# First chunk pair of the first group as eight plain block products, with the sums of x and of the weights due later

## The reference

```python
def lora_add(base, inp, A, B):
    Ab = A[layer_idx][lora_indices]
    Bb = B[layer_idx][lora_indices]
    t = jnp.einsum('bri,bni->bnr', Ab, inp)
    return base + jnp.einsum('bor,bnr->bno', Bb, t) * SCALE
gate = lora_add(jnp.einsum('bnh,fh->bnf', x, W_gate), x, A_gate, B_gate)
up = lora_add(jnp.einsum('bnh,fh->bnf', x, W_up), x, A_up, B_up)
act = jax.nn.silu(gate) * up
down = lora_add(jnp.einsum('bnf,hf->bnh', act, W_down), act, A_down, B_down)
...
logits = x @ W_gate + b_gate
_, top_idx = jax.lax.top_k(logits, TOP_K)
y_all = jax.nn.relu(jnp.einsum('bsd,edh->bseh', x, W_e) + b_e)
y = jnp.take_along_axis(y_all, top_idx[..., None], axis=2)
return y.mean(axis=2)
```

## Time and profile before

| | |
|---|---|
| median of 3 runs | 1849.49 us (1849.46 to 1853.57) |
| the profiled execution, its own time | 1849.29 us |
| its span | 1847.4 us |
| PE busy | 1811.7 us, 98% of the span |
| DVE / ACT / POOL busy | 1252.5 / 751.6 / 1078.5 us |
| mean granted TensorE clock | 0.995 |
| DMA | 350.33 MB, 190 GB/s on average |

### The profile page before, as it was taken

How to read it: one execution, slowest core, us unless ns; L and a number is a source line. 1 busy time by engine, 2 the same in 40 slices (tenths; PEclk the granted TensorE clock), 3 DMA queues, 4 the chain that set the end, 5 groups by cost and what they waited for, 6 DMA issues and landing times.

```text
span 1847.4 us, 25090 instructions
## 1 busy us (share of the span) xinstructions
PE 1811.7 (98%) x8582; PEld 1507.1 (82%) x8582; DVE 1252.5 (68%) x1496; ACT 751.6 (41%) x1128; POOL 1078.5 (58%) x676
## 2 busy tenths in 40 slices
PE   7999999999999999999999999999999999999997
PEld 6788888888888888888888888888888888888886
DVE  8877788875567797888888886477788642234400
ACT  5544444444543335444444444443323333333332
POOL 2678888873434445545656553444433776676664
PEclk9999999999999999999999999999999999999999
DMA  5556665644667655565566665567635876577643
GB/s 211 173 200 225 223 205 202 234 171 147 208 230 249 223 181 184 174 195 179 179 201 210 191 207 189 191 232 243 219 117 180 244 192 145 141 193 186 157 103 47
DMA packets 128396, 350.33 MB, mean 190 GB/s; under 512 B 15232, under 2 KB 17152, under 8 KB 128000
## 3 DMA queue, kind: packets, MB, share of 16 engines
q1 hardware_dynamic: 110320, 286.94, 45.7%
q0 software_dynamic: 17952, 61.75, 14.3%
HBM read 267.49 MB, written 90.05 MB: 194 GB/s over the span
## 4 chain that ended last, share of the span: by engine, by line
PE 82%; POOL 8%; DMA 3%; DVE 3%; issue 2%; ACT 1%; SPq 0%; POOLq 0%; ACTq 0%; DVEq 0%
PE PS L1716 25%; PE PS L1717 25%; PE PS L1718 25%; PE PS L1831 2%; PE PS L2059 2%; PE PS L1758 2%; DMA FT<-in_wp 1%; POOL FT L719 1%; POOL ytp L715 1%; POOL FT L717 1%; POOL FT L693 1%; POOL brw L749 1%; POOL ytp L713 1%; POOL FT L688 1%; DMA X<-in_xp 1%
## 5 line engine op out<-in xcount | busy, mean ns | idle before, releaser
L1716 PE MATMUL PS<-R,ring 128*128 128x512 f32 (+1 forms) x1800 | 708.5, 394 | 18.7 <-DVE R L937 9.4
L1717 PE MATMUL PS<-R,ring 128*128 128x512 f32 (+1 forms) x1800 | 703.5, 391 | 0.0
L1718 PE MATMUL PS<-R,ring 128*128 128x512 f32 (+1 forms) x1800 | 702.6, 390 | 0.0
L1716 PEld LDWEIGHTS PS<-R,ring 128*128 128x128 f32 x1800 | 339.3, 189 | 88.6 <-issue 12.8
L1718 PEld LDWEIGHTS PS<-R,ring 128*128 128x128 f32 x1800 | 339.1, 188 | 72.0
L1717 PEld LDWEIGHTS PS<-R,ring 128*128 128x128 f32 x1800 | 339.7, 189 | 65.9
L770 POOL TENSOR_TENSOR ring<-raw,ring 128x1024 fp32r<-128x1024 f32 x78 | 192.7, 2471 | 267.7 <-ACT ring L893 267.6
L1716 PE MATMUL PS<-ring,R 128*128 128x512 f32 x592 | 231.7, 391 | 1.7 <-DVE FT L1234 1.7
L1717 PE MATMUL PS<-ring,R 128*128 128x512 f32 x592 | 230.8, 390 | 0.0
L1718 PE MATMUL PS<-ring,R 128*128 128x512 f32 x592 | 230.4, 389 | 0.0
L749 POOL DMA_INDIRECT brw<-in_bgu,idx_b x88 | 94.0, 1068 | 226.9 <-DVE R L1058 187.9
(11 more groups left out here) (189 smaller groups left out, 2365.8 us busy)
## 6 DMA issues: line engine op xcount, KB each, us to landing
raw<-in_wp SPq DMA_DIRECT2D x124, 512.0 KB
act_scratch<-FT SPq DMA_DIRECT2D x140, 256.0 KB, 5.0
FT<-act_scratch SPq DMA_DIRECT2D x70, 512.0 KB, 4.4
raw<-in_we SPq DMA_DIRECT2D x64, 512.0 KB
ytp<-in_wgb SPq DMA_DIRECT2D x96, 256.0 KB, 4.8
raw<-wt_scratch SPq DMA_DIRECT2D x40, 512.0 KB
out<-in_xn SPq DMA_DIRECT2D x17, 512.0 KB, 5.5
y_scratch<-FT SPq DMA_DIRECT2D x7, 1024.0 KB, 6.0
```

Source lines behind the costliest of these rows:

```text
L1716: e.matmul(out_, hi, whi, start=start, stop=False, skip_group_check=True)
L1717: e.matmul(out_, hi, wlo, start=False, stop=False, skip_group_check=True)
L1718: return e.matmul(out_, lo, whi, start=False, stop=stop, skip_group_check=True)
```

## The change

The first group's first chunk pair (q = 0) is made of eight plain block products, which need no sums at all, summed in PSUM: banks 0 and 1 take two products each with B11 and B21, banks 2 and 3 two each with B12 and B22. Gate results then lie complete in four banks; silu reads them there (`plain_silu`), and the four copies and four additions of this pair go. The other seven products of q = 1 follow after all eight. x is split in the order B11, B21, B12, B22, T1, T2, T3, T4; B12 lies in the place that T3 takes later, so the high part of T3 now waits until the plain products with B12 and `lora1_in(0, 1)` are through. `lora1_in(0, 1)` takes B12 and B22 (32 small matmuls) instead of T1, B11 and B22 (48). The third weight block is now issued after all of x. The due times of the first 14 slots are written in microseconds through `early`.

```diff
-X_FIRST = ["B11", "B21", "T1", "T2", "B22", "T3", "T4"]
+X_FIRST = ["B11", "B21", "B12", "B22", "T1", "T2", "T3", "T4"]
+PLAIN = [(0, "B11", 0), (1, "B21", 0), (2, "B11", 1), (3, "B21", 1), (0, "B12", 2), (1, "B22", 2), (2, "B12", 3), (3, "B22", 3)]
...
+def pos(g, q, j):
+
+    if g == 0:
+        return 7 * q + j if q >= 2 else 4 + j
...
+def early(us):
+
+    return (us - 9.4) / 3.57 - 1
...
-        sp.add(-23.5, load, 2)
+        sp.add(-20.5, load, 2)
...
             elif r == 5:
-                e.wait_ge(s_xl, 14)
+                e.wait_ge(s_xl, 16)
...
+            if g == 0 and o == "T3":
+                e.wait_ge(s_pe, 3)
+                e.wait_ge(s_t1, 2)
             if g == 0 and o == "T4":
                 e.wait_ge(s_xl, x_at(0, "T3", 1))
...
-        def mix_w0(e, q, part):
+        def mix_w0(e, part):
...
         def e_copy(e, g, q, k):
...
-            if q and k == 0:
+            if g == 0 and q == 1 and k < 2:
+                if k == 0:
+                    e.wait_ge(s_gl, 4)
+                    e.wait_ge(s_as, AS_FIRST)
+            elif q and k == 0:
                 e.wait_ge(s_c, c_of(g, q - 1, 2))
...
+        def plain_silu(e, k):
+
+            if k == 0:
+                e.wait_ge(s_p0, 1)
+                e.wait_ge(s_xp, 4)
+                e.wait_ge(s_xl, x_at(0, "T2", 1))
+            e.activation(tile(SG_T + k), PS[:, [0, 2, 1, 3][k], :], ACT.Silu).then_inc(s_c, 1)
...
+        W_HI = [5.4, 9.0, 12.3, 12.9, 21.8, 21.9, 26.6, 32.5, 36.0, 49.2, 49.3]
...
+        X_LO = {"B11": (7.5, 8.5), "B21": (10.5, 11.5), "B12": (14.0, 15.0), "B22": (16.5, 17.5),
+                "T1": (24.0, 24.1), "T2": (32.0, 32.1), "T3": (41.0, 41.1), "T4": (50.0, 50.1)}
...
-                src = ([("B11", 0), ("B21", 4)], [("T1", 0), ("B11", 0), ("B22", 4)])[w]
+                src = ([("B11", 0), ("B21", 4)], [("T1", 0), ("B11", 0), ("B22", 4)] if g else [("B12", 0), ("B22", 4)])[w]
...
+            def plain(i):
+
+                n, x, bank_ = PLAIN[i]
+                e.wait_ge(s_lo, lo_of(0, n))
+                m = main1(0, n, x, bank_, i % 2 == 0)
+                if i >= 4:
+                    m.then_inc(s_pe, 1)
...
             def first_pairs(g):
+                if g == 0:
+                    for i in range(4):
+                        plain(i)
+                    lora1_in(0, 0)
+                    for i in range(4, 8):
+                        plain(i)
+                    lora1_in(0, 1)
+                    lora1_out(0, 0, 0, 0, 0)
+                    lora1_out(0, 0, 1, 0, 1)
+                    product(0, 1, 0)
+                    product(0, 1, 1)
+                    lora1_out(0, 0, 0, 1, 2)
+                    lora1_out(0, 0, 1, 1, 3).then_inc(s_p0, 1)
+                    for j in range(2, 7):
+                        product(0, 1, j)
+                    return
```

More of the change, by code:

```diff
@@ L80, in pos, with when_at @@
     return 7 * q + j
-AT_POS = {pos(q, j): (q, j) for q in range(NP) for j in range(7)}
+def when_at(g, q, j):
+    return 7 + j if g == 0 and q == 1 else pos(g, q, j)
+def early(us):
+    return (us - 9.4) / 3.57 - 1
+AT_POS = [{pos(g, q, j): (q, j) for q in range(1 - g, NP) for j in range(7)} for g in range(2)]
 def op(g, n):
@@ L105, in piece_list @@
             n0 = op(g, 7 * q)
-            first, second = {0: (-6.0, -5.5), 1: (-12.7, -6.0)}.get(q, (-6.0, -5.5))
+            first, second = {0: (-6.0, -5.5), 1: (-12.7 if g else -12.3, -6.0)}.get(q, (-6.0, -5.5))
             out.append((n0 + first, ("w", g, 2 * q)))
@@ L261, in build @@
         s_v = sem("s_v")
+        s_p0 = sem("s_p0")
         s_m, s_oe = sem("s_m"), sem("s_oe")
@@ L592, in build @@
                     free = op(a, 148) - 4.7
+                elif a == 0 and q < 2:
+                    free = early([[11.5, 14.5], [36.5, 53.0]][q][c])
                 elif c:
-                    free = op(a, pos(q, 6)) - 4.7
+                    free = op(a, pos(a, q, 6)) - 4.7
                 else:
@@ L953, in x0_t3 @@
             e.wait_ge(s_xt, h + 1)
+            e.wait_ge(s_xl, x_at(0, "B12", h))
             e.wait_ge(s_q[6 + h], 16)
@@ L1343, in block0_lo @@
                             ALU.subtract).then_inc(s_tlo, 1)
+        W_HI = [5.4, 9.0, 12.3, 12.9, 21.8, 21.9, 26.6, 32.5, 36.0, 49.2, 49.3]
+        W_LO = [6.1, 10.0, 13.0, 13.1, 23.0, 23.1, 31.6, 39.5, 39.6, 48.5, 51.5]
+        X_HI = {"B11": (6.5, 7.5), "B21": (9.5, 11.0), "B12": (13.6, 14.6), "B22": (15.6, 16.6),
+                "T1": (22.0, 22.1), "T2": (30.5, 30.6), "T3": (40.0, 40.1), "T4": (47.0, 47.1)}
+        X_LO = {"B11": (7.5, 8.5), "B21": (10.5, 11.5), "B12": (14.0, 15.0), "B22": (16.5, 17.5),
+                "T1": (24.0, 24.1), "T2": (32.0, 32.1), "T3": (41.0, 41.1), "T4": (50.0, 50.1)}
         for g in range(NG):
             for n in range(LO1):
+                if g == 0 and n < 14:
+                    if n < 11:
+                        act.add(early(W_HI[n]), w_hi, 0, n)
+                        dve.add(early(W_LO[n]), w_lo, 0, n)
+                    continue
                 key = op(g, n) - (4.98 if g == 0 or n > 4 else 4.96 if n % 2 else 3.98)
+                if g == 0 and n < 20:
+                    key = n - 1.95 if n < 17 else 14.05 + 0.3 * (n - 17)
                 act.add(key, w_hi, g, n)
@@ L1396, in build @@
                 for k in range(4):
[L1397 to L1399 removed]
+                    if (g, q) == (0, 0):
+                        act.add(early(48.7 + 0.1 * k), plain_silu, k)
+                        continue
+                    key = 9.2 if g and q == 1 and k == 0 else when_at(g, q, [0, 2, 3, 5][k]) + 1.05
                     act.add(op(g, key), e_copy, g, q, k)
[L1401 removed]
+                    due = op(g, when_at(g, q, [4 if q < 2 else 1, 6, 6, 6][k]) + [1.1, 1.05, 1.1, 1.15][k])
                     dve.add(due, c_add, g, q, k)
@@ L1438, in build @@
         for h in range(2):
-            dve.add(-1.75 + 0.001 * h, x0_t1, h)
-            dve.add(-0.8 + 0.001 * h, x0_t2, h)
-            dve.add(1.2 + 0.001 * h, x0_t3, h)
-            dve.add(2.2 + 0.001 * h, x0_t4, h)
-        for q in range(2):
-            for part in range(3):
-                dve.add([[-1.5, 0.16, 1.16], [2.5, 2.51, 2.52]][q][part], mix_w0, q, part)
+            dve.add(early(20.5 + 0.1 * h), x0_t1, h)
+            dve.add(early(29.0 + 0.1 * h), x0_t2, h)
+            dve.add(early(37.0 + 0.1 * h), x0_t3, h)
+            dve.add(early(45.5 + 0.1 * h), x0_t4, h)
+        for part in range(3):
+            dve.add(early([26.5, 35.0, 35.1][part]), mix_w0, part)
         for k in range(8):
```

143 lines of the change are left out of this document (69 added, 74 removed).

## The result

The changed kernel took 1858.54 us (median of 6 runs, 1854.53 to 1860.3), the kernel before 1849.47 us beside it (6 runs, 1848.69 to 1853.57): ratio 1.0043, 95% interval 1.0029 to 1.0057. It is slower by about 9 us (by the interval, 5 to 11), 0.6 us over the forecast and inside the range. The profiled execution took 1860.3 us, its span is 1858.5 us. It is the slowest of the six, 1.8 us above their median, so what it shows late in the program need not be typical.

What follows compares the result with a forecast made beforehand. PE, busy 98%, bounds the kernel. The chain gave +8.4 us, PE's account (work +0.9, waits 16.0 against 7.6) +9.3; 8.6 was taken on 1849.29, forecasting 1857.9, with 1851.0 to 1862.0 for 8 in 10.

Steps and rivals of the forecast that it cites:

- PE's own work: Before q = 2: one more product, 2.75 us, and 16 fewer small adapter matmuls, minus 1.8; sum +0.9 us.
- First wait: Before the adapter's product: PE waits 1.8 us, until 23.9, for the adapter's low parts, now behind both halves of B22.
- Second and third: PE's waits before q = 2: 2.2 us for the B rows, until 50.4, and 1.0 us for product 4's copy, at 57.3.
- The chain: From the adapter product through T3, T4, ACT's silus to T4's low part at 61.9, then POOL's gather and last copy, 76.9.
- POOL's piece: From the start of q = 2's weight sums (63.4) to the gathered rows' high part (75.2): 11.8 us, unchanged.
- The clock: After PE's long wait before q = 2: 3.4 us at half rate, losing 1.7 us, the same price as before.
- Nothing later: Behind the long wait, later weight high parts and gathers are late by as much as PE and hold up nothing more.
- A: Faster: T4's low part by 50.9 us, last copy not late: 1845.0, or 1839.9 without the first three waits; chance 0.06.
- B: About the same: POOL's chain only half as late, T4 between 52 and 58: 1848 to 1855, typically 1852; chance 0.16.
- C: Slower still: gather for pairs 2 and 3 late, table switch with drain: +1 to +3, up to 1861.5; chance 0.10.
- D: Before q = 2: the third sum's copy isn't needed that early; rejected in the prediction, no size or chance given.

Runs made afterwards that it cites:

- the fastest version: Changed kernel with second row gather, silus, adapter's low parts and gathered rows moved, POOL's q = 2 weight sums held until T4: 1843.73 us, 0.9958 of kernel before.

## Why the prediction was right

**PE's own work, +0.9.** By PE's account the front grew by 6.6 us of waits and 0.8 us more lost to the clock, and 7.65 in all, so the rest is +0.3, 0.6 less than forecast. Some 0.45 of these are no work of the change: PE ended its first four products at 21.82 instead of 22.27, though they use the same blocks, because its first matmuls went over to the faster pace 0.9 us earlier in this execution (see the last section). So the term itself was about right.

**First wait.** Predicted 1.8 us and PE going on at 23.9; measured 2.01 and 23.83. The time at which PE goes on is the forecast that held; the length of the wait was 0.5 to 2.0 us in the seven profiles that share this stretch of the program, and PE went on at 23.8 to 23.9 in all of them.

**Second and third.** 2.2 at 50.4 and 1.0 at 57.3; measured 2.20 at 50.39 and 0.83 at 57.41.

**The chain.** First half of T3's high part at 45.9, measured 45.83; T4 written at 53.3, measured 53.33; ACT's split done at 54.4, measured 54.43; high part of the weight block 58.9, measured 58.8; T4's low part 61.9, measured 61.8. Every length was read off the same operation in the rows before, and the order from the due times. From the start of the table load to the start of the first silu it took 1.30 us, against 1.29 in the earlier trace rows. The Trainium skill ("ScalarE: Activation LUTs", What ACT_TABLE_LOAD costs) adds a drain of 1.38 us, which is in neither trace, though ACT had just ended a split (52.23 + 2.20 = 54.43) when the load began.

**POOL's piece, 11.8 us, was the mis-sized term.** The sums started at 63.32 (63.4 predicted), and the high part of the gathered rows at 73.76 instead of 75.2: 10.4 us. The sums took 5.9 us instead of the 6.8 that the kernel before had shown beside a busy DVE, the first of the two gathers took 0.9 instead of 1.2, and the high part began 3.16 us after the second gather's start instead of 3.4. I had put the first at up to 1 us and not taken it. So PE waited 9.1 us instead of 11 and went on at 75.45 instead of 76.95.

**The clock.** Predicted 3.4 us of work at half the rate, 1.7 lost. PE came back at 75.45 with the clock already down (0.50 from 70.2 us on, while it waited) and ran at half until 80.4: 5 us, 2.5 lost. This made up for part of the term above: 7.65 at the end of q = 2 where I had 8.6.

**Nothing later: wrong.** I took a free quarter of POOL and PE at work in the earlier trace rows as proof that no later stage would add to it. The same queue at 320 us had a wait of 0.4 us in the kernel before. It became 1.7 us and a fall of the clock in one profile of the changed kernel, and was 0.4 us without a fall in the other. That the forecast's 1857.9 came within 0.6 us of the measured 1858.5 is partly luck: the front was forecast 1 us too dear, and what came after it was put at nothing; and the same kernel measured again gave 1856.75. The mechanism, one late job that holds up POOL's list up to the last copy, is what the prediction had right.

**The rivals.** A and B needed T4's low part by 50.9 or by 52 to 58; it came at 61.8. C's late gather and drain did not come. D is excluded by the run with the copy ahead: with the copy made early, PE did its last four small matmuls without a wait. What A promised, 1845.0 with the long wait gone and 1839.9 with all waits gone, is near to what the fastest version reaches (1843.73), with waits of 2.20, 0.37 and 1.15 left before q = 2 and the one of 1.3 behind it; but that version also has the gathered rows later, which A did not count.

## What to carry to other kernels

Where an engine runs a fixed list, follow the job that the change makes late through every list that it stands in. Here the waits that the change removed were worth 6.7 us, and a gather of rows for the second group, made late, cost about 8, because weight sums stood behind it. The same holds for the repair: the stores that went back with the gather made the next gathers late and cost a new wait of 1.3 us. When one wait is taken away, look what the engine that is freed starts earlier, and beside whom: POOL's sums beside DVE's low parts cost 2 us, which an added wait on POOL won back.

## What the runs showed of the hardware

**Two engines' additions slow each other.** POOL's additions of 128 x 512 took 1.3 us while DVE was idle (three of 1.27 to 1.29 in the last run with the sums held) and 2.1 beside DVE; of DVE's two halves of T3's low part in the run with the gather moved, one took 2.31 us instead of 1.22. That is longer by 1.1 us, near the 1.3 us of one addition of POOL's. With the sums held back both halves together took 2.36 again. The Trainium skill ("SBUF — State Buffer", Who interferes with whom) says that a DVE instruction with two inputs in SBUF contends with a POOL instruction that reads SBUF, over ports that only one of them has at a time; the trace agrees that both become longer.

**The same short wait does not always cost the same clock.** After the wait of 2.20 us near 50 us the clock stayed at 1.00 in both profiles of the changed kernel and fell to half for over 3 us in the runs with the silus, the copy or the gathered rows moved. These edits touch only jobs behind this wait, so the difference lies between executions and not in the program. In every profile PE comes to eight matmuls of only 8 columns after 0.25 us of idle near 1390 us:

```profile
1388.24 1.06 PE L1977 MATMUL PS<-wg_s,ytp 128*128 128x8 f32 x8 [0.25 <-ACT ytp L1250]
```

That is the kernel before. Behind it the clock was at half for 7 us there, about 10 in the changed kernel, about 14 in the fastest version, and not at all in the run with the gathered rows later; in 5 of the 13 profiles it did not fall. The program is the same at this place in all of them. This loses between 0 and 7 us, which is as wide as the effect of the change; what decides it was not tried, and that the narrow matmuls bring it about is not shown.

**The start of PE scatters too.** The first matmuls of 128 x 512 start 0.43 us apart and later ones 0.23 us apart. The change of pace came at 13.2 us in the profile of the kernel before, at 12.3 us in that of the changed kernel and at 15.4 us in that of the run with the gather moved, whose program is the same as the changed kernel's up to there. So PE ended its first four products at 21.82 and at 23.27 us, and its wait for the adapter, which ended at 23.8 in both, was 2.0 us in the one and 0.5 in the other.
